# GNN and FFN kernel: the tail's residual arithmetic moved from GpSimd to VectorE, LayerNorm 4 put into the tile loop

## The chip, the core and the metric

The kernel runs on one core of one Trainium2 chip. The core has a TensorE (matrix products, called PE in the profile), a VectorE (DVE), a ScalarE (ACT), a GpSimd (POOL) and a SyncE that issues transfers (SP). The metric is the device time of one execution in microseconds (us). The engines run their own instruction streams in order and meet only at semaphores, so an engine that waits also holds up everything that stands behind the wait in its own stream.

## What is computed

6250 nodes of 256 features pass four steps, each with a residual: a weighted sum over 106250 edges, a mixture of experts, a two-layer graph convolution and a feed-forward network on the best-scored half of the nodes. The change lies in the second convolution's product, its LayerNorm (called LN5 here), and what the last step needs ahead of its network:

```
h = _gcn_conv(x, src, dst, W1, b1); h = relu(h)
h = _gcn_conv(h, src, dst, W2, b2)      # (segment sum) @ W2, * deg_in**-0.5, + b2
h = _layer_norm(h, gamma, beta)         # LN5
x = x + h                               # residual
n = _layernorm(x)                       # LN4
weights = n @ wr + br                   # router score of each node
idx = top_k(weights, k)                 # half of the nodes
x = x + (n, plus y * score for the chosen rows, y = ffn(n))
```

The reference reads "x = x + L1_ffn(n)" with "processed + n" inside, so the output of a node that is not chosen is x + n.

## The kernel before

The nodes lie as 49 tiles (T) of 128 rows in seven chunks (NCH) of seven tiles (CH). X is the residual stream, 128 x 49 x 256 in SBUF (in reg_a). ACC (in reg_b) is 128 x 49 x 257: 256 features and one column that counts edges.

**The convolutions** (tags p1 and p2) work block by block: GpSimd gathers the rows of 128 edges with an indirect DMA (`gathers`, L629, 831 of them for each convolution, into a ring of 24 slots), SyncE relays the arrivals, ScalarE makes one-hot matrices (L787, L797), TensorE multiplies (L1780) into eight PSUM banks in turn, and VectorE adds the result to its tile of ACC (L1324 in `item_sums`, 880 items).

**The tile loops** (tags c1 and c2) follow each convolution: for each tile TensorE transposes ACC (L1690), ScalarE copies the transposed tile out of PSUM (`evacuate`, L755), TensorE multiplies with the weights (L1700), and VectorE scales by the degree and adds the bias (`product`, L1448). In c1 ScalarE applies relu (L809) and SyncE writes the rows to HBM, from where p2 gathers them. GpSimd may start p2's gathers only when all of these rows are written. Ahead of c1 VectorE takes the edge counts (L1441) and inverts their square root.

**The tail** is everything from c2 to the router scores WV. LN5 is spread over VectorE (`ln_stats` L843 and L846, `ln_scale` L851 to L870) and ScalarE (`ln_std` L684, `ln_apply` L693) chunk by chunk within the c2 loop. GpSimd then multiplies the chunk by gamma (L664) and adds it to X (L666); it had added beta to the whole of X between the gathers of p1 and p2 (L655). After the loop LN4 runs in the same way over X, GpSimd adds the normalized chunk to X for the output (L670), and VectorE takes the 49 score products with the router's weights (L1482), plus the bias (L1484). A search for the threshold, the inversion of the selection, and the network follow (L1498 onwards).

The order on every engine is the order of the code. What sets it around the change are the positions `t % CH` in the loops at which the pieces of a LayerNorm are issued.

Of the kernel before, what the change touches and what calls it, by code (L numbers as in the profile page):

```python
# [14 lines left out]
P = 128  # L15
ALU = mybir.AluOpType
# [37 lines left out]
def gnn_program(nc, x, src, dst, edge_weight, Wr, br, ln_g, ln_b, W1, b1, W2, b2,  # L54
# [6 lines left out]
    KC = D // P  # L61
# [39 lines left out]
    with ExitStack() as ctx:  # L101
# [145 lines left out]
        gws = tb[:, 0:2 * KC * D].rearrange("p (l c d) -> p l c d", l=2, c=KC)  # L247
        GB1B, GB2B, GAMB, BETB, FB2B, FWRB = (tb[:, 2 * KC * D + k * D:2 * KC * D + (k + 1) * D] for k in range(6))
# [35 lines left out]
        CNTS = sm(7)  # L284
        EDGE = sm(3).bitcast(I32)
# [117 lines left out]
        def _(sp):  # L403
# [88 lines left out]
            for l, a in enumerate((gW1, gW2)):  # L492
                sp.dma_start(gws[:, l, :, :], a.rearrange("(c p) d -> p c d", p=P)).then_inc(z("tail_in"), 16)
            for to, a in ((GB1B, gb1), (GB2B, gb2), (GAMB, gamma), (BETB, beta), (FB2B, fb2)):
                sp.dma_start(to, row1(a, D)).then_inc(z("tail_in"), 16)
# [44 lines left out]
        def _(pool):  # L540
# [92 lines left out]
            def chunk(c):  # L633
                w_ = slice(c * CH, (c + 1) * CH)
                return X[:, w_, :], ACC[:, w_, 0:D]


# [15 lines left out]
            pool.wait_ge(z("tail_in"), 8 * 16)  # L653
            pool.wait_ge(*norms("ln3", "norm", NCH))
            g.tensor_tensor(X, X, per_column(BETB, T), ALU.add).then_inc(z("beta_in"), 1)  # L655
# [3 lines left out]

            pool.wait_ge(z("beta_in"), 1)  # L660
            for c in range(NCH):
                x_, h = chunk(c)
                pool.wait_ge(*norms("ln5", "norm", c + 1))
                g.tensor_tensor(h, h, per_column(GAMB, CH), ALU.mult).then_inc(z("scaled"), 1)  # L664
                pool.wait_ge(z("scaled"), c + 1)
                g.tensor_tensor(x_, x_, h, ALU.add).then_inc(z("x3_set"), 1)  # L666
            for c in range(NCH):
                x_, h = chunk(c)
                pool.wait_ge(*norms("ln4", "norm", c + 1))
                g.tensor_tensor(x_, x_, h, ALU.add).then_inc(z("sum_set"), 1)  # L670
# [7 lines left out]
        def _(act):  # L678
# [135 lines left out]
            for t in range(T):  # L814
                if t + 1 < T:
                    evacuate("c2", t + 1)
                c = t // CH - 1
                if c >= 0 and t % CH == 2:
                    ln_std("ln5", c)
                if c >= 0 and t % CH == 5:  # L820
                    ln_apply("ln5", c, *[lambda i: ACC[:, c * CH + i, 0:D]] * 2)
# [1037 lines left out]
```

## Time and profile before

| what | us |
|---|---|
| runs | 5300.11, 5294.97, 5300.14 (median 5300.11) |
| profiled execution | 5287.03 |
| its span, first to last instruction | 5285.4 |
| busy: PE, DVE, ACT, POOL | 3767.5, 2195.0, 1831.9, 2937.5 |

Around the span lie 1.6 us of the profiled execution. The profiled execution is 13.1 us (0.25%) under the median of the three runs. The page gives busy time by engine, the costliest groups of instructions (line, engine, operation, names and shapes, then busy time, mean ns of one, and idle time just before), and the chain that ended last. The places of this change were read from the timeline (start, duration, engine, line, with the idle time before in brackets and what ended it) and from the table of stretches.

### The profile page before, as it was taken

To read this page: it belongs to the slowest core of one execution; us is meant where nothing else is said; L and a number is where in the kernel's file an instruction comes from. 1 tells how busy PE (TensorE), PEld (TensorE's weight loads), DVE (VectorE), ACT (ScalarE), POOL (GpSimd) and SP (SyncE) were. 2 spreads that over 40 slices of the span, in tenths; PEclk is the share of its full clock that TensorE was granted. 3 is DMA by queue.
4 is the path that set the end of the run, shared out by engine and by line. 5 is a ranking of instruction groups with operands and counts; after the bars stand their busy time and mean duration, and the time that the engine had idled before them with its cause. 6 is when DMAs were issued, how large, how long until landed. Compare 5 with 4: busy or idle time off the path is not lost.

```text
span 5285.4 us, 63030 instructions
## 1 busy us (share of the span) xinstructions
PE 3767.5 (71%) x14313; PEld 2762.7 (52%) x14313; DVE 2195.0 (42%) x6079; ACT 1831.9 (35%) x4499; POOL 2937.5 (56%) x2860
## 2 busy tenths in 40 slices
PE   1666668986886999999566666666666666666178
PEld 0444447765666688888433443333433433345167
DVE  8543336665775411111333333334433333334831
ACT  5333333332003522222344444443444444443331
POOL 0677777776000133333277777777377777775413
PEclk9888889998996999999767777777877778778579
DMA  2334347776886244444533333333233333332212
GB/s 80 117 123 124 122 137 244 243 244 200 251 249 217 65 109 111 116 108 109 143 108 106 105 106 106 105 106 96 88 106 106 106 105 106 105 105 68 97 22 31
DMA packets 322627, 660.22 MB, mean 125 GB/s; under 512 B 60683, under 2 KB 142923, under 8 KB 322150
## 3 DMA queue, kind: packets, MB, share of 16 engines
q0 software_dynamic: 148960, 365.25, 23.9%
q1 hardware_dynamic: 173318, 290.95, 18.5%
q8 instruction: 142, 2.33, 0.2%
q14 instruction: 207, 1.70, 0.1%
HBM read 488.94 MB, written 174.87 MB: 126 GB/s over the span
## 4 chain that ended last, share of the span: by engine, by line
POOL 30%; issue 10%; PE 6%; DVE 3%; DMA 1%; ACT 1%; SPq 0%; POOLq 0%; DVEq 0%; ACTq 0%
POOL work L629 30%; PE bank L1728 2%; PE bank L1700 2%; PE bank L1739 2%; DVE small L843 0%; DMA conv_rows<-work 0%; DVE work L1482 0%; PE bank L1761 0%; DVE small L1441 0%; PE bank L1690 0%; DVE work L1516 0%; ACT reg_b L693 0%; SPq L491 0%; DMA out_dram<-work,slot_t 0%; ACT work L693 0%
## 5 line engine op out<-in xcount | busy, mean ns | idle before, releaser
L1780 PE MATMUL bank<-work,reg_a 128*128 x3520 | 1349.7, 528 | 808.5 <-DVE reg_b L1324 359.4
L629 POOL DMA_INDIRECT work<-conv_rows,tables x1662 | 1571.6, 946 | 618.1 <-issue 505.7
L1780 PEld LDWEIGHTS bank<-work,reg_a 128*128 128x128 f32 x3520 | 820.1, 254 | 1338.1 <-issue 1220.7
L1324 DVE TENSOR_TENSOR reg_b<-reg_b,bank 128x257 f32 x1760 | 744.2, 423 | 1336.1 <-PE bank L1780 1232.8
L590 POOL DMA_INDIRECT messages<-work,small x880 | 883.0, 1003 | 292.7 <-issue 184.5
L797 ACT ACTIVATE reg_a<-reg_a,ones 128x512 f32<-128x512 f32 x440 | 317.7, 722 | 1155.5 <-PE bank L1780 1155.1
L1639 PE MATMUL bank<-reg_b,reg_a 128*128 x1760 | 539.4, 449 | 242.1 <-ACT work L720 216.8
L720 ACT ACTIVATE work<-bank,tables 128x256 f32<-128x256 f32 x880 | 387.2, 473 | 784.7 <-PE bank L1639 387.4
L787 ACT ACTIVATE reg_a<-iota,tables 128x128 f32<-128x128 f32 x1760 | 562.5, 391 | 31.3 <-DVEq L1457 12.8
L1639 PEld LDWEIGHTS bank<-reg_b,reg_a 128*128 128x128 f32 x1760 | 352.3, 218 | 376.2 <-issue 334.6
L611 POOL DMA_INDIRECT residual_rows<-work,slot_t x112 | 177.8, 1588 | 478.8 <-DVE work L1303 306.6
L601 POOL DMA_INDIRECT work<-expert_in_rows,slot_t x112 | 111.8, 998 | 526.1 <-DVEq L1265 473.4
L1728 PE MATMUL bank<-work,reg_a 128*128 128x256 f32 x1792 | 397.8, 381 | 2.5 <-DVE work L1285 2.5
L1652 PE MATMUL bank<-reg_b,reg_a 128*128 128x257 f32 x1544 | 369.7, 387 | 27.8 <-DVE reg_a L1185 27.7
L1728 PEld LDWEIGHTS bank<-work,reg_a 128*128 128x128 f32 x1792 | 342.1, 191 | 49.3 <-DVE work L1285 3.1
L1652 PEld LDWEIGHTS bank<-reg_b,reg_a 128*128 128x128 f32 x1544 | 291.4, 192 | 90.0 <-DVE reg_a L1185 49.6
L747 ACT ACTIVATE work<-bank,param_t 128x256 f32<-128x256 f32 x280 | 117.3, 470 | 362.7 <-PE bank L1728 362.6
L747 ACT ACTIVATE tables<-bank,param_t 128x256 f32<-128x256 f32 x272 | 114.0, 470 | 359.6 <-PE bank L1728 359.6
L1195 DVE TENSOR_TENSOR reg_a<-reg_a,bank 128x257 f32 x514 | 215.6, 419 | 47.1 <-PE bank L1652 29.0
L1185 DVE TENSOR_TENSOR reg_a<-iota,tables 128x512 f32<-128x512 f32 x257 | 177.8, 692 | 102.2 <-PE bank L1652 76.7
L1285 DVE TENSOR_SCALAR work<-bank,param_t 128x256 f32<-128x256 f32 x112 | 55.8, 539 | 345.5 <-PE bank L1715 345.4
L1739 PE MATMUL bank<-reg_b,tables 128*128 x896 | 198.0, 379 | 0.0
(341 smaller groups left out, 3745.0 us busy)
## 6 DMA issues: line engine op xcount, KB each, us to landing
reg_b<-messages SPq DMA_DIRECT2D x386, 258.0 KB, 3.5
reg_a<-in_L_ffn_W_dram SPq DMA_DIRECT2D x56, 1024.0 KB, 5.3
b_rows<-messages SPq DMA_DIRECT2D x128, 258.0 KB
reg_a<-item_rows SPq DMA_DIRECT2D x110, 256.0 KB, 3.8
work<-conv_rows,tables POOLq DMA_INDIRECT x1662, 2.7
messages<-work,small POOLq DMA_INDIRECT x880
conv_rows<-work SPq DMA_DIRECT2D x14, 896.0 KB, 4.0
reg_b<-in_L_ffn_W_dram SPq DMA_DIRECT2D x8, 1024.0 KB, 11.8
```

Source lines behind the costliest of these rows:

```text
L590: g.indirect_dma_start(msgs, bass.IndirectOffsetOnAxis(ap=PIDX[:, i % 32:i % 32 + 1], axis=0), G[:, u, :], None, bounds_check=BASE2 + E2 - ...
L629: g.indirect_dma_start(GC[:, u, 0:D], None, table, bass.IndirectOffsetOnAxis(ap=BSRC[:, b_:b_ + 1], axis=0)).then_inc(z(f"conv_in{u // 4}" ...
L720: a.activation(G[:, u, 0:D], ps[i % 3][:, 0:D], ACT.Copy, scale=WT[:, i:i + 1]).then_inc(z("m_row"), 1)
L747: a.activation(HT[j % 2][:, k, :], ps[1 + k // 2][:, k % 2 * PP:(k % 2 + 1) * PP], gelu, bias=PT[:, bass.ds(col, 1)]).then_inc(z("net_gelu ...
L787: ins = a.activation(DIST[:, k % 8, :], IOTA[:], ACT.Abs, bias=DREL[:, k:k + 1], scale=-1.0)
L797: a.activation(OHP[:, i % OHR:i % OHR + 4, :], DIST[:, i % 8:i % 8 + 4, :], ACT.Relu, scale=-1.0, bias=ONES[:, 0:1]).then_inc(z("conv_oh"), 4)
L1324: v.tensor_tensor(acc, acc, ps[i % 8][:, 0:D + 1], ALU.add).then_inc(z("conv_add"), 1)
L1639: pe.matmul(ps[i % 3][:, 0:D], OHT[:, i % 8, :], XNf[:, bass.ds(offs[k], D)], start=True, stop=True).then_inc(z("m_mm"), 1)
L1652: pe.matmul(ps[sum_bank(pr)][:, 0:D + 1], SOH[:, q % 2 * 4 + b_, :], QG[q % 4][:, b_, 0:D + 1], start=(k == 0), stop=(k == 1)).then_inc(z( ...
L1728: ins = pe.matmul(ps[1 + k // 2][:, k % 2 * PP:(k % 2 + 1) * PP], w_, XE[:, c, :], start=(c == 0), stop=(c == KC - 1))
L1739: ins = pe.matmul(ps[5 + j % 2][:, h * D:(h + 1) * D], HT[j % 2][:, k, h * P:(h + 1) * P], w_, start=(k == 0), stop=(k == HC - 1))
L1780: pe.matmul(ps[i % 8][:, 0:D + 1], OHP[:, i % OHR, :], GCf[:, bass.ds(offs[i % 4], D + 1)], start=True, stop=True).then_inc(z(f"{tag}_mm"), 1)
```

## The change

Beta is now added by VectorE, one tile at a time, inside the c1 loop. Gamma and the residual add are now done by VectorE, one chunk at a time, inside the c2 loop. LN4 runs two chunks behind the products in that same loop, which has two more rounds of seven steps. x + n, which is x (1 + r) - mean r, is one ScalarE activation per tile (`sums`) in place of GpSimd's add. The scores are no longer taken from the normalized rows. They are assembled from parts: an extra 257th weight column (W2 times gamma times wr, summed) gives the score part of h out of the c2 product, and X times wr is summed per tile. The 55 VectorE steps that make these parts (`score_parts`) are placed in `item_sums` of p2, one after every eighth item.

```
-            g.tensor_tensor(X, X, per_column(BETB, T), ALU.add).then_inc(z("beta_in"), 1)
...
-                g.tensor_tensor(h, h, per_column(GAMB, CH), ALU.mult).then_inc(z("scaled"), 1)
-                g.tensor_tensor(x_, x_, h, ALU.add).then_inc(z("x3_set"), 1)
...
-                g.tensor_tensor(x_, x_, h, ALU.add).then_inc(z("sum_set"), 1)
```

ScalarE:

```
+            def sums(c):
+                for t in range(c * CH, (c + 1) * CH):
+                    ins = a.activation(X[:, t, :], X[:, t, :], ACT.Identity, bias=NB[:, 1, t:t + 1], scale=RS1[:, t:t + 1])
+                ins.then_inc(z("sum_set"), 1)
+            for t in range((NCH + 2) * CH):
                 if t + 1 < T:
                     evacuate("c2", t + 1)
+                c5, c4, at = t // CH - 1, t // CH - 2, t % CH
+                if 0 <= c5 < NCH and at == 0:
+                    ln_std("ln5", c5)
+                if 0 <= c5 < NCH and at == 1:
+                    ln_apply("ln5", c5, *[lambda i: ACC[:, c5 * CH + i, 0:D]] * 2)
+                if c4 >= 1 and at == 3:
+                    sums(c4 - 1)
+                if c4 >= 0 and at == 4:
+                    ln_std("ln4", c4, 1)
+                if c4 >= 0 and at == 6:
+                    ln_apply("ln4", c4, ...)
```

VectorE:

```
+            def score_parts():
+                step(v.tensor_tensor(GFB, GAMB, FWRB, ALU.mult))
+                for c in range(KC):
+                    step(v.scalar_tensor_tensor(DUMP, GW2X[:, c, 0:D], 1.0, GFB, ALU.mult, ALU.mult,
+                                                accum_out=GW2X[:, c, D:D + 1]))
...
+                for t in range(T):
+                    step(v.scalar_tensor_tensor(DUMP, X[:, t, :], 1.0, FWRB, ALU.mult, ALU.mult, accum_out=WV[:, t:t + 1]))
+                    yield
...
+                    if side is not None and i % 8 == 6:
+                        next(side, None)
...
+                v.tensor_tensor(X[:, t, :], X[:, t, :], BETB, ALU.add).then_inc(z("beta_in"), 1)
...
+            for t in range((NCH + 2) * CH):
+                if t < T:
+                    product("c2", D + 1, t, ACC[:, t, :], GB2X).then_inc(z("lin2"), 1)
+                c5, c4, at = t // CH - 1, t // CH - 2, t % CH
+                if 0 <= c5 < NCH:
+                    if at == 0:
+                        ln_stats("ln5", c5, lambda i: ACC[:, c5 * CH + i, 0:D])
+                    if at == 1:
+                        ln_scale("ln5", c5)
+                if c4 >= 0:
+                    if at == 0:
+                        residual(c4)
+                    if at == 2:
+                        step(v.tensor_tensor(X[:, w_, :], X[:, w_, :], ACC[:, w_, 0:D], ALU.add))
+                    if at == 3:
+                        ln_stats("ln4", c4, lambda i: X[:, c4 * CH + i, :], 1)
+                    if at == 5:
+                        ln_scale("ln4", c4, 1, plus_one=RS1)
```

`residual(c)` waits for LN5's applied chunk c and multiplies it by gamma. The order on GpSimd between the gathers, before (L655 is the beta add, L664 and L666 the first of gamma and residual):

```order
L629 DMA work<-conv1_rows,tables 128x256 x831
L655 TENSOR_TENSOR reg_a<-reg_a,reg_b 128x49x256
L629 DMA work<-conv2_rows,tables 128x256 x831
L664 TENSOR_TENSOR reg_b<-reg_b 128x7x256
L666 TENSOR_TENSOR reg_a<-reg_a,reg_b 128x7x256
```

and now:

```order
L633 DMA work<-conv1_rows,tables 128x256 x831
L633 DMA work<-conv2_rows,tables 128x256 x831
L605 DMA work<-ffn_in_rows,slot_t 128x256 x8
```

GpSimd computes nothing any more between the first gather of p1 and the network. On VectorE, the step from one chunk to the next in the c2 loop before (L1448 is the product, L843 and L846 LN5's statistics, L862 to L870 its scale):

```order
L1448 SCALAR_TENSOR_TENSOR reg_b<-bank5,small,reg_b 128x256
L843 BN_STATS small<-reg_b 128x6 x7
L846 BN_AGGR small<-small 128x2 x7
L1448 SCALAR_TENSOR_TENSOR reg_b<-bank2,small,reg_b 128x256
```

and one whole chunk of the c2 loop now (L1463 is the product, L1481 gamma, L1498 the residual add, L860 one plus the scale; L832 with reg_b is LN5's statistics, with reg_a LN4's):

```order
L1463 SCALAR_TENSOR_TENSOR reg_b<-bank3,small,reg_b 128x257
L832 BN_STATS small<-reg_b 128x6 x7
L835 BN_AGGR small<-small 128x2 x7
L1481 TENSOR_TENSOR reg_b<-reg_b 128x7x256
L1463 SCALAR_TENSOR_TENSOR reg_b<-bank4,small,reg_b 128x257
...
L1463 SCALAR_TENSOR_TENSOR reg_b<-bank5,small,reg_b 128x257
L1498 TENSOR_TENSOR reg_a<-reg_a,reg_b 128x7x256
L1463 SCALAR_TENSOR_TENSOR reg_b<-bank2,small,reg_b 128x257
L832 BN_STATS small<-reg_a 128x6 x7
L835 BN_AGGR small<-small 128x2 x7
```

Gamma, the residual add and LN4 have moved between the products, and the product of a tile waits its turn behind them. In p2 a side step (L1312) now stands between two of VectorE's item adds (L1336):

```order
L1336 TENSOR_TENSOR reg_b<-reg_b,bank6 128x257
L1312 SCALAR_TENSOR_TENSOR reg_b<-reg_b 128x256
L1336 ISA
L1336 TENSOR_TENSOR reg_b<-reg_b,bank7 128x257
```

One such step follows every eighth add, 55 in all, so they end at item 440 of 880.

## Rows read from the trace of the kernel before

**Rows 1.** The page's costliest groups: GpSimd's gathers of both convolutions

```profile
L629 POOL DMA_INDIRECT work<-conv_rows,tables x1662 | 1571.6, 946 | 618.1 <-issue 505.7
```

**Rows 2.** Table of stretches: us, busy (x) of PE, PEld, DVE, ACT, POOL, granted clock, DMA

```profile
3716.00:3777.00 61.00, 58.75 (x277) 43.82 (x275) 22.72 (x47) 36.21 (x94) 0.00 (x0) 1.00 0.27 91
4700.00:4825.00 125.00, 79.94 (x222) 50.63 (x222) 46.52 (x110) 43.45 (x108) 90.76 (x96) 0.80 0.36 103
...
4845.00:4852.00 7.00, 5.97 (x16) 4.74 (x17) 3.73 (x16) 2.29 (x7) 6.05 (x2) 0.51 0.00 0
4852.00:4910.00 58.00, 39.71 (x191) 31.91 (x189) 34.34 (x133) 29.31 (x71) 32.76 (x10) 0.94 0.00 1
4910.00:4999.00 89.00, 0.00 (x0) 0.00 (x0) 85.53 (x245) 29.76 (x64) 42.63 (x11) 0.50 0.42 144
```

**Rows 3.** Timeline (start, us, engine, line) where p1 ends and c1 begins

```profile
3685.94 24.51 POOL L655 TENSOR_TENSOR reg_a<-reg_a,reg_b 128x12544 f32<-128x12544 f32 x1
...
3691.76 18.76 DVE L1441 TENSOR_SCALAR small<-reg_b 128x49 f32<-128x49 f32 x1
```

**Rows 4.** Timeline of the c1 loop: two products, and p2's first gather

```profile
3719.17 0.48 DVE L1448 SCALAR_TENSOR_TENSOR work<-bank,small,reg_b 128x256 f32<-128x256 f32 x1 [0.70 <-PE bank L1700]
...
3720.57 0.48 DVE L1448 SCALAR_TENSOR_TENSOR work<-bank,small,reg_b 128x256 f32<-128x256 f32 x1 [0.91 <-PE bank L1700]
...
3781.30 0.97 POOL L629 DMA_INDIRECT work<-conv_rows,tables  x1 [70.85 <-DMA conv_rows<-work]
```

**Rows 5.** Timeline of the message stage: GpSimd's DMA issues beside VectorE's operations

```profile
903.00 0.56 DVE L1108 TENSOR_TENSOR reg_a<-reg_a,work 128x392 f32<-128x392 f32 x1
...
910.31 0.41 DVE L1195 TENSOR_TENSOR reg_a<-reg_a,bank 128x257 f32 x1
910.36 0.97 POOL L590 DMA_INDIRECT messages<-work,small  x1 [0.30 <-issue]
...
911.26 0.69 DVE L1185 TENSOR_TENSOR reg_a<-iota,tables 128x512 f32<-128x512 f32 x1
911.63 1.17 POOL L590 DMA_INDIRECT messages<-work,small  x1 [0.30 <-issue]
```

**Rows 6.** Timeline of the c2 loop, around the first two LN5 chunks

```profile
4825.18 0.42 DVE L1324 TENSOR_TENSOR reg_b<-reg_b,bank 128x257 f32 x1 [0.20 <-DVE reg_b L1324]
...
4835.74 2.37 DVE L843 BATCH_NORM_STATS2 small<-reg_b 128x6 f32<-128x256 f32 x7
...
4838.64 1.23 DVE L1448 SCALAR_TENSOR_TENSOR reg_b<-bank,small,reg_b 128x256 f32<-128x256 f32 x3
...
4840.94 0.19 DVE L862 RECIPROCAL small<-small 128x7 f32<-128x7 f32 x1
...
4842.18 3.55 ACT L693 ACTIVATE reg_b<-reg_b,small 128x256 f32<-128x256 f32 x7 [1.04 <-DVE small L870]
...
4846.03 2.08 PE L1700 MATMUL bank<-reg_b,work 128*128 128x256 f32 x4 [3.13 <-ACT work L755]
...
4859.93 1.13 PE L1700 MATMUL bank<-reg_b,work 128*128 128x256 f32 x4 [3.14 <-ACT work L755]
```

**Rows 7.** VectorE's groups from 4825.6 to 4999: busy us, mean ns

```profile
L1482 DVE SCALAR_TENSOR_TENSOR work<-reg_b 128x256 f32<-128x256 f32 x49 | 28.1, 573 | 1.7
...
L870 DVE SCALAR_TENSOR_TENSOR small<-small 128x7 f32<-128x7 f32 x14 | 20.6, 1470 | 0.5
...
L853 DVE TENSOR_SCALAR small<-small 128x7 f32<-128x7 f32 x14 | 9.7, 692 | 0.5
```

**Rows 8.** Timeline of GpSimd and of VectorE in LN4: one add beside one scale

```profile
4933.05 3.97 POOL L670 TENSOR_TENSOR reg_a<-reg_a,reg_b 128x1792 f32<-128x1792 f32 x1 [4.09 <-ACT reg_b L693]
```

```profile
4933.23 3.81 DVE L870 SCALAR_TENSOR_TENSOR small<-small 128x7 f32<-128x7 f32 x1
```

**Rows 9.** Timeline of VectorE at the end of the tail

```profile
4968.68 0.42 DVE L1482 SCALAR_TENSOR_TENSOR work<-reg_b 128x256 f32<-128x256 f32 x1
...
4998.84 0.25 DVE L1484 TENSOR_SCALAR small<-small,brb 128x49 f32<-128x49 f32 x1
```

More of the change, by code:

```diff
@@ L813, in _ @@
             evacuate("c2", 0)
[L814 removed]
+            def sums(c):
[3 more added lines that the diff above has]
+            for t in range((NCH + 2) * CH):
                 if t + 1 < T:
                     evacuate("c2", t + 1)
[L817 to L821, printed above, removed]
[L822 to L829 removed]
+                c5, c4, at = t // CH - 1, t // CH - 2, t % CH
[8 more added lines that the diff above has]
+                if c4 >= 0 and at == 6:
+                    ln_apply("ln4", c4, lambda i: X[:, c4 * CH + i, :], lambda i: ACC[:, c4 * CH + i, 0:D], 1)
+            sums(NCH - 1)
             scale_onehots("ffn", NFT, T, lambda s, t: WV[:, t:t + 1])
@@ L869, in ln_scale @@
                     step(v.tensor_tensor(r, r, extra[:, w_], ALU.mult))
+                if plus_one is not None:
+                    v.tensor_scalar(plus_one[:, w_], r, 1.0, None, ALU.add)
                 v.scalar_tensor_tensor(n, MV[:, s, w_, 0], -1.0, r, ALU.mult, ALU.mult).then_inc(norms(tag, "scale")[0], 1)
@@ L1444, in _, with product @@
             v.wait_ge(z("tail_in"), 8 * 16)
-            def product(tag, l, t, to, bias):
+            v.wait_ge(*norms("ln3", "norm", NCH))
+            def product(tag, width, t, to, bias):
                 v.wait_ge(z("tile_mm"), t + 1 + TILES_BEFORE[tag])
-                return v.scalar_tensor_tensor(to, ps[2 + t % 4][:, 0:D], DI[:, t:t + 1], bias, ALU.mult, ALU.add)
+                return v.scalar_tensor_tensor(to, ps[2 + t % 4][:, 0:width], DI[:, t:t + 1], bias, ALU.mult, ALU.add)
             for t in range(T):
@@ L1457, in _ @@
             v.engine_nop().then_inc(z("conv_ready"), 1)
-            item_sums("p2")
+            item_sums("p2", score_parts())
             v.wait_ge(z("conv_add"), 2 * NI)
-            for t in range(T):
-                product("c2", 1, t, ACC[:, t, 0:D], GB2B).then_inc(z("lin2"), 1)
-                c = t // CH - 1
-                if c >= 0 and t % CH == 0:
-                    v.wait_ge(z("lin2"), (c + 1) * CH)
-                    ln_stats("ln5", c, lambda i: ACC[:, c * CH + i, 0:D])
-                if c >= 0 and t % CH == 4:
-                    ln_scale("ln5", c)
@@ L1487, in _ @@
+            step(v.scalar_tensor_tensor(T1, MV[:, 1, :, 0], MINUS_F, WV, ALU.mult, ALU.add))
+            step(v.tensor_tensor(T1, T1, RS[:, 1, :], ALU.mult))
+            step(v.tensor_scalar(WV, T1, FBR, None, ALU.add))
             ROUND = [0]
```

83 lines of the change are left out of this document (36 added, 47 removed).

## Prediction

> **What bounds the kernel now.** I read the costliest groups first, then the table of stretches, then the timeline at the three places that the change touches. The convolutions are bound by GpSimd: a gather is busy 946 ns and 505.7 us of issue gaps are spread over 1662 of them, so (1571.6 + 505.7) / 1662 = 1.25 us each, without a wait on anything else [rows 1]. VectorE has room there: 46.5 us busy in 125 [rows 2].
>
> At the end of p1 the reader should see a 49-column operation of VectorE, L1441, that takes 18.76 us, while GpSimd's addition of beta runs from 3685.94 for 24.51 us. Both end at 3710.5 [rows 3]. An operation of this width takes 0.25 us elsewhere (L1484) [rows 9]. It stands ahead of c1, whose rows p2's gathers wait for (70.85 us idle) [rows 4], so its length is on the path.
>
> The tail runs from the last item add, which ends at 4825.60 [rows 6], to the score bias at 4998.84 [rows 9]: 173.2 us. The same collision is in it. An LN4 scale started at 4933.23, 0.18 us behind GpSimd's add, and ended with it [rows 8]. A seven-column operation needs under 0.2 us (L862: 0.19) [rows 6] and a score product 0.42 [rows 9]. With 0.17 for the first kind the stall is L870 20.6 - 2.4 = 18.2, L853 9.7 - 2.4 = 7.3, L1482 28.1 - 20.6 = 7.5, together 33 us [rows 7].
>
> **The change part by part.**
>
> *Beta leaves GpSimd.* L1441 falls from 18.76 to about 0.25 us: **-18.5 us**, and all of c1 and p2 moves up by it. What is late next is the reciprocal chain and the first copy, which came right behind L1441 anyway. GpSimd's own gathers do not wait less, since c1's rows release them.
>
> *Beta on VectorE, 49 adds of 128x256 in c1.* From 0.56 us for 392 columns and 0.69 for 512, both with two SBUF inputs [rows 5], one column costs 1.1 ns and 256 columns cost 0.41 us. c1's products start 1.40 and 1.18 us apart and take 0.48 [rows 4], and the cycle is product, relu, copy, TensorE. 0.48 + 0.41 = 0.89 us fits into the shorter step, so this costs **0**; VectorE ends c1 0.4 us later, but p2's first gather needs the written rows only. Uncovered it would be 20 us.
>
> *The 55 side steps in p2.* VectorE has the time. The danger is GpSimd. An issue that began at 911.63, inside an operation of VectorE with two SBUF inputs (911.26 to 911.95), took 1.17 us in place of 0.97; one that began at 910.36 inside an operation with one input in PSUM took 0.97 [rows 5]. p2's own adds are of the second kind, 53 of the side steps of the first. A gather starts inside a 0.42 us step one time in three (0.42 / 1.25), and then loses half of it less 0.1, so 53 x 0.05 = **+3 us**. The low bound is 0, where no start falls inside; the high one is 53 x 0.42 = 22, where each does.
>
> The Trainium skill, "SBUF — State Buffer", "Who interferes with whom", says that a two-input `tensor_tensor` takes only the read interface of the shared ports, that descriptor generation needs the write interface, and so (inferred, it says) that DMA issue is not stalled. By that rule this term would be 0; the stretched issue speaks against it.
>
> *The tail.* No arithmetic of GpSimd is left beside VectorE, so the 33 us of stalls go, and so do the 49 score products (4968.68 to 4998.84, 30 us, of which 7.5 are stall [rows 7, 9]). In exchange VectorE gets 14 operations of 128x1792. At 0.56 + 1400 x 1.1 ns that is 2.05 us each (GpSimd took about 4 [rows 8]); an upper end is 2.4, if all of the 512-column row's 0.69 us scaled with the width, and a lower one 1.8, if a tenth of the slope is lost to overlap. The walk below moves by +3 and -2 us between them, since the residual add stands beside a wait.
>
> I walked through one full chunk of the new order, with 0.4 us for a product (three take 1.23), 2.9 for statistics (2.37 plus the seven small ones), 1.1 for a scale (4840.94 until ScalarE starts at 4842.18, less 0.1), 3.55 for seven applied tiles, and 1.13 + 0.4 us for TensorE and the copy [rows 6]:
> - product 0.4, LN5 statistics 2.9, gamma 2.05, product 0.4, LN5 scale 1.1: 6.9 us
> - ScalarE has meanwhile stopped at `ln_apply`, and the copies of the coming tiles stand behind it. Two products were ready and the residual add (2.05) runs beside it; then VectorE waits: apply 3.55, copy and TensorE 1.5, about 5.1 us from the scale to the next product
> - product 0.4, LN4 statistics 2.9, product 0.4, wait 0.4, product 0.4, LN4 scale 1.2, product 0.4, wait 0.3: 6.4 us
>
> That is 18.4 us a chunk, of which VectorE waits 3.7 or so; before, the products behind two applies in turn were 13.9 us apart (4846.03 to 4859.93). The loop has 10.1 us for chunk 0 as before (4825.60 to 4835.74), 14.5 for chunk 1 (LN5 only, its scale now holds the copies early), 4 x 18.4 + 17.5 for the next five, 14.7 for round 7 (no products: statistics twice 2.9, gamma and add 4.1, scales 2.3, 2.5 of waiting for ScalarE's `apply` and `sums`), 9.5 for round 8, and 0.8 for the last three small operations: **141 us** with TensorE at the full clock. The same walk of the old order, with GpSimd's operations holding VectorE, gives 172.6 against the 173.2 seen, so I trust it to a few us.
>
> *TensorE's clock.* The tile products took 1.13 us at 4859.93 and 2.08 at 4846.03 [rows 6], the latter in a stretch at 0.51, behind a wait of 3.13 us. From 4852 to 4910 the granted clock was 0.94 with TensorE busy 68%, in the convolution 0.80 at 64% [rows 2]. In the new loop TensorE has 7 x 1.13 = 7.9 us of work in 18.4, or 43%. At the half level throughout the walk gives 168 us, since each of a chunk's three waits for a tile grows by about 1 us and chunk 0 by 8. I take a mixture, full in the first chunk and half in about half of the others: **148 us, so -25**.
>
> Sum: -18.5 + 0 + 3 - 25 = -40.5, so 5287.0 - 40.5 = 5246.5 for an execution like the profiled one. The median of the runs is 13.1 us above it, so 5300.1 - 40.5 = **5259.6, say 5259**.
>
> **The rivals.**
> - *Full clock in the tile loop*: 141 us, gain 18.5 + 32 - 3, time 5252, down to 5243 if the big operations are at their low end. For it: 1.00 in c1 at dense work [rows 2]. Against it: TensorE's idle stretches of 3 to 6 us in each chunk.
> - *Half clock in the tile loop*: 168 us, gain 18.5 + 5 - 3, time 5280. For it: the stretch at 0.51; against it: the next wait of 3.14 us was followed by a product at 1.13.
> - *The side steps hold up GpSimd for whole issues*: the end on the other side. If VectorE's two-input step and a gather take turns so that each step costs GpSimd one gather of 1.25 us, the 53 cost 66 us, and the time is 5300.1 - 43.5 + 66 = 5323. It decides from 43.5 / 53 = 0.82 us a step. Against it: the stretched issue lost 0.20 us, and VectorE's operation in progress there had its usual 0.69 [rows 5]. A milder form, 0.3 us for each, gives 5273.
> - *The new loop eats the gain*: if GpSimd's share only moves to VectorE at GpSimd's price (4 us for each of the 14), the chunk grows by 4 us, the tail is 168 to 176, and the time 5282 to 5290. Against it: the 1.1 ns a column.
>
> **How the numbers follow.** The mixed clock (5253 to 5270) 0.5; full clock or better (5240 to 5253) 0.2; half clock or a mild side cost (5270 to 5287) 0.2; GpSimd's price 0.04; whole issues lost 0.04; the rest 0.02. The range takes the first three but their outer ends: 5241 to 5283. About 0.2% (10.6 us) can be told from no change; the L1441 stall alone is worth more. Faster 0.91, same 0.05, slower 0.04.
>
> **What would show it.** L1441's successor at 0.25 us, c1 starting within 1 us of the last item add, and c1's products still 2.58 us apart by twos. GpSimd's gathers in the first half of p2 at 1.25 us with some at 1.1 to 1.4; p2 from first gather to last item add 3 us longer than 4825.6 - 3781.3 = 1044.3. Rounds of 18 to 20 us in the c2 loop, with VectorE's longest wait for TensorE behind each LN5 apply; no VectorE operation of seven columns over 0.2 us; last item add to score bias 141 to 155 us; everything behind as before. I am wrong if c1 shows products further apart, if 128x1792 takes over 2.4 us, or if the granted clock in the loop is 0.5.

## The result, and the profile after

The changed kernel took 5253.43 us (median of 4, 5242.20 to 5255.98) and the kernel before, run beside it, 5298.39 (5294.97 to 5300.14). The ratio is 0.9913 with a 95% interval of 0.9899 to 0.9928: 45.0 us less, where 40.5 were predicted; the time itself was put at 5259 us, in a range of 5241 to 5283. The profiled execution has a span of 5240.6 us against 5285.4, 44.8 less. The two traces divide it like this (each stretch by its first and last rows):

| stretch | before | after | difference | predicted |
|---|---|---|---|---|
| start to the end of p1's last item add | 3691.72 | 3691.11 | -0.6 | 0 |
| from there to c1's first product | 21.67 | 2.30 | -19.4 | -18.5 |
| c1, first product to last | 62.55 | 61.93 | -0.6 | 0 |
| to p2's first gather | 5.36 | 5.35 | 0 | 0 |
| p2, first gather to last item add | 1044.30 | 1046.97 | +2.7 | +3 |
| last item add to the start of the score bias | 173.24 | 147.19 | -26.1 | -25 |
| the rest | 286.5 | 285.8 | -0.8 | 0 |

The first and the last row, which the change doesn't touch, show that two executions differ by some 0.8 us in such a stretch anyway. GpSimd is less busy and TensorE, VectorE and ScalarE about as much as before. The gathers still bound the convolutions, at the same cost of issue. First the page of the kernel after, busy time by engine (us) and the group of the gathers, which answers to [rows 1]:

```profile
PE 3780.5 (72%) x14313; PEld 2766.9 (53%) x14313; DVE 2181.9 (42%) x6165; ACT 1853.8 (35%) x4548; POOL 2837.6 (54%) x2838
...
L633 POOL DMA_INDIRECT work<-conv_rows,tables x1662 | 1574.0, 947 | 622.3 <-issue 505.7
```

**The end of p1.** The timeline after (start, us, engine, line) answers to [rows 3] and [rows 4]; L1455 is the operation that was L1441, L1463 the product and L1468 the beta add:

```profile
3691.15 0.20 DVE L1455 TENSOR_SCALAR small<-reg_b 128x49 f32<-128x49 f32 x1
...
3692.13 1.13 PE L1726 MATMUL bank<-reg_b,work 128*128 128x256 f32 x4 [0.24 <-ACT work L739]
...
3693.41 0.48 DVE L1463 SCALAR_TENSOR_TENSOR work<-bank,small,reg_b 128x256 f32<-128x256 f32 x1 [0.27 <-PE bank L1726]
3693.81 0.41 DVE L1468 TENSOR_TENSOR reg_a<-reg_a,reg_b 128x256 f32<-128x256 f32 x1
```

```profile
3760.69 0.94 POOL L633 DMA_INDIRECT work<-conv_rows,tables  x1 [75.41 <-DMA conv_rows<-work]
```

The 49-column operation takes 0.20 us where it took 18.76, and c1 starts at once. The beta add takes the 0.41 us that was worked out from [rows 5], and the products of c1 are still 2.58 us apart by twos (3716.61, 3719.19, 3721.77). GpSimd's idle time before p2 is longer than in [rows 4] (75.41 against 70.85) because it now has nothing to compute there.

**The side steps in p2.** In the timeline after, three of GpSimd's gathers and one side step (L1312) that the middle one started inside:

```profile
3796.00 0.95 POOL L633 DMA_INDIRECT work<-conv_rows,tables  x1 [0.30 <-issue]
...
3797.18 0.42 DVE L1312 SCALAR_TENSOR_TENSOR reg_b<-reg_b 128x256 f32<-128x256 f32 x1
3797.25 1.17 POOL L633 DMA_INDIRECT work<-conv_rows,tables  x1 [0.30 <-issue]
...
3798.72 0.95 POOL L633 DMA_INDIRECT work<-conv_rows,tables  x1 [0.30 <-issue]
```

From 3760 to 4310, the half with side steps, 16 of 438 gathers took 1.01 to 1.17 us, and each of these started inside a side step with two SBUF inputs; in the same half of the kernel before the longest gather took 0.97. Together the 16 are 2.4 us over 0.947 each. How long each took follows from where in the step of 0.42 us it started: 0.07 us in it took 1.17 us, 0.14 in 1.09 to 1.10, 0.23 in 1.01, and the five that started 0.28 us in or later took 0.94 to 0.95. That is what a gather looks like that is held until about 0.3 us after the start of the step, 0.1 before its end, as the prediction assumed. The 16 include the one `tensor_tensor` among the side steps (L1309): a gather that started 0.11 us into it took 1.13.

**The c2 loop.** One round of seven steps runs from one gamma multiplication (L1481) to the next. The timeline after, with one LN5 apply (L677), answers to [rows 6]:

```profile
4837.37 2.00 DVE L1481 TENSOR_TENSOR reg_b<-reg_b 128x1792 f32<-128x1792 f32 x1
...
4856.70 1.99 DVE L1481 TENSOR_TENSOR reg_b<-reg_b 128x1792 f32<-128x1792 f32 x1
...
4860.36 3.55 ACT L677 ACTIVATE reg_b<-reg_b,small 128x256 f32<-128x256 f32 x7 [2.98 <-DVE small L861]
4860.64 2.02 DVE L1498 TENSOR_TENSOR reg_a<-reg_a,reg_b 128x1792 f32<-128x1792 f32 x1
4863.81 0.62 ACT L739 COPY work<-bank 128x256 f32<-128x256 f32 x2
...
4864.21 2.08 PE L1726 MATMUL bank<-reg_b,work 128*128 128x257 f32 x4 [5.43 <-ACT work L739]
...
4866.41 0.49 DVE L1463 SCALAR_TENSOR_TENSOR reg_b<-bank,small,reg_b 128x257 f32<-128x257 f32 x1 [3.76 <-PE bank L1726]
```

ScalarE applies LN5 to seven tiles, the copy of the next tile stands behind it, TensorE has been idle for 5.43 us and runs that tile at 2.08 us in place of 1.13, and VectorE waits 3.76 us for it. VectorE's groups from 4838 to 4986 (busy us, mean ns) answer to [rows 7]:

```profile
L1498 DVE TENSOR_TENSOR reg_a<-reg_a,reg_b 128x1792 f32<-128x1792 f32 x7 | 14.1, 2018 | 0.0
L1481 DVE TENSOR_TENSOR reg_b<-reg_b 128x1792 f32<-128x1792 f32 x7 | 14.0, 1996 | 0.0
...
L842 DVE TENSOR_SCALAR small<-small 128x7 f32<-128x7 f32 x13 | 2.2, 170 | 0.4
```

The wide operations take 2.00 and 2.02 us, half of what one took on GpSimd [rows 8]. L842, which was L853 with a mean of 692 ns, takes 170: no seven-column operation is held up any more. Table of stretches after (us, busy (x) of PE, PEld, DVE, ACT, POOL, granted clock), which answers to [rows 2]:

```profile
3693.40:3755.40 62.00, 58.33 (x285) 44.74 (x284) 39.27 (x97) 36.54 (x95) 0.00 (x0) 1.00 0.27 90
...
4833.00:4851.00 18.00, 9.87 (x38) 7.30 (x36) 13.36 (x43) 5.85 (x16) 0.00 (x0) 0.72 0.01 1
4851.00:4870.00 19.00, 10.50 (x42) 8.05 (x42) 14.23 (x50) 12.65 (x30) 0.00 (x0) 0.82 0.20 69
4870.00:4889.00 19.00, 11.83 (x39) 9.18 (x40) 14.23 (x50) 12.80 (x30) 0.00 (x0) 0.73 0.27 92
```

c1 ran at full clock, the c2 loop at 0.72 to 0.82 in these stretches. The tail ends with the score bias, which answers to the last line of [rows 9]:

```profile
4954.85 0.25 DVE L1510 TENSOR_SCALAR small<-small,brb 128x49 f32<-128x49 f32 x1
```

### The profile page after: what moved, and what is told of

The parts are those of the page before. It is cut to its first block and busy times, and to the rows that moved or that the text cites. A ratio compares the mean times of both kernels' runs of the same rounds, so it can differ in the third digit from the quotient of the medians.

```text
span 5240.6 us, 63145 instructions
## 1 busy us (share of the span) xinstructions
PE 3780.5 (72%) x14313; PEld 2766.9 (53%) x14313; DVE 2181.9 (42%) x6165; ACT 1853.8 (35%) x4548; POOL 2837.6 (54%) x2838
## 5 line engine op out<-in xcount | busy, mean ns | idle before, releaser
L1336 DVE TENSOR_TENSOR reg_b<-reg_b,bank 128x257 f32 x1760 | 744.1, 423 | 1319.2 <-PE bank L1806 1212.0
L1678 PE MATMUL bank<-reg_b,reg_a 128*128 128x257 f32 x1544 | 371.6, 388 | 26.1 <-DVE reg_a L1176 26.0
## 6 DMA issues: line engine op xcount, KB each, us to landing
reg_b<-in_L_ffn_W_dram SPq DMA_DIRECT2D x8, 1024.0 KB, 11.8
```

The lines of the kernel that those rows point to most:

```text
L1336: v.tensor_tensor(acc, acc, ps[i % 8][:, 0:D + 1], ALU.add).then_inc(z("conv_add"), 1)
L1678: pe.matmul(ps[sum_bank(pr)][:, 0:D + 1], SOH[:, q % 2 * 4 + b_, :], QG[q % 4][:, b_, 0:D + 1], start=(k == 0), stop=(k == 1)).then_inc(z( ...
```

## The experiments

The kernels ran in three groups, each with the kernel before beside it: 5291.7 us in the first, 5901.28 in the second, 5859.33 in the third. In the last two the convolutions were slower (GpSimd also waited for free ring slots), so times are compared within a group only. The result above is a measurement apart. "Tail" below is the time from the last item add to the end of the score bias: 173.5 us before, 147.4 after. It contains no gathers and differs less between the groups: of the kernels with the order of the changed one, e3, e4 and e10 of the last two groups have 148.7 to 149.6.

### Beta: who holds up whom

**e1_beta_only** (first group) is the kernel before with nothing changed but beta:

```
-            g.tensor_tensor(X, X, per_column(BETB, T), ALU.add).then_inc(z("beta_in"), 1)
...
                 product("c1", 0, t, ZB[:, t % 2, :], GB1B).then_inc(z("lin1"), 1)
+                v.tensor_tensor(X[:, t, :], X[:, t, :], BETB, ALU.add).then_inc(z("beta_in"), 1)
```

> The kernel before with one part of the change alone: beta is added by VectorE in c1, tile by tile, and GpSimd keeps gamma, residual and the last add. Theory (the 18.76 us of L1441 were GpSimd's one long addition): the edge-count operation takes 0.2 us, c1 starts right behind the last item add, the time falls by 18 to 20 us, ratio to before 0.9964. The tail stays at 173 us. Rival (the gain at this place in the changed kernel came from less work elsewhere): under 5 us.

Measured: 5272.41 us, 0.9962 [0.9948, 0.9975], 19.3 us less. The 49-column operation took 0.20 us, the tail 172.7. Beta alone is worth what the first term of the sum said.

**e2_beta_pieces** (first group) leaves beta on GpSimd, in 49 pieces:

```
-            g.tensor_tensor(X, X, per_column(BETB, T), ALU.add).then_inc(z("beta_in"), 1)
+            for t in range(T):
+                g.tensor_tensor(X[:, t, :], X[:, t, :], BETB, ALU.add).then_inc(z("beta_in"), 1)
```

> The kernel before with GpSimd's addition of beta cut into 49 additions of 128x256. The work stays on GpSimd and still overlaps VectorE; only the length of one instruction changes. Theory (GpSimd holds the port for one instruction at a time, and VectorE gets in between): the edge-count operation waits at most one piece, 0.6 us, and the time falls by 15 to 20 us, ratio about 0.9966, although GpSimd needs longer for the whole, some 30 us. Rival (VectorE is slow or starved as long as GpSimd computes at all): it still takes over 10 us, and the gain is under 8 us.

Measured: 5298.19 us, 1.0011 [1.0002, 1.0020], 6.5 us more than before, about as much as the pieces take longer together than one addition (31.26 against 24.51). It was to wait for one piece and waited for all. The timeline of GpSimd and of VectorE in this kernel:

```profile
3690.66 31.26 POOL L656 TENSOR_TENSOR reg_a<-reg_a,reg_b 128x256 f32<-128x256 f32 x49
```

```profile
3696.59 25.39 DVE L1442 TENSOR_SCALAR small<-reg_b 128x49 f32<-128x49 f32 x1
```

The pieces take 31.26 us and VectorE's operation, begun 5.9 us in, ends with the last of them. The Trainium skill, "SBUF — State Buffer", "SBUF: two separate sides", has it that the one of the two that starts first keeps the shared ports for the whole instruction. Read as one instruction at a time, that would have let VectorE in after one piece, 0.64 us (31.26 / 49); in this trace the end of an instruction is not enough when the next one is ready.

**e9_beta_waits** (third group) is e2 with a wait between the pieces:

```
                 g.tensor_tensor(X[:, t, :], X[:, t, :], BETB, ALU.add).then_inc(z("beta_in"), 1)
+                pool.wait_ge(z("beta_in"), t + 1)
```

> The kernel before with GpSimd's beta in 49 additions, and GpSimd waiting on a semaphore for each before it issues the next. In the version without these waits VectorE's edge-count operation was held for 25.39 us, until the last of the 49. Theory (VectorE gets the port only where GpSimd has nothing issued, which a wait gives): the edge-count operation takes under 1.2 us, c1 starts 1 to 2 us behind the last item add, the time falls by 15 to 19 us, ratio 0.9968. Rival (VectorE's operation is served last whatever GpSimd's queue looks like): again over 20 us, ratio 1.000 or more.

Measured: 5855.81 us, 0.9995 [0.9986, 1.0004]. The mechanism came out, the time did not: the interval is from 8 us faster to 2 us slower. GpSimd and VectorE in its timeline:

```profile
4090.87 0.95 POOL L629 DMA_INDIRECT work<-conv_rows,tables  x1 [0.30 <-issue]
4091.83 37.33 POOL L656 TENSOR_TENSOR reg_a<-reg_a,reg_b 128x256 f32<-128x256 f32 x49
```

```profile
4109.77 0.34 DVE L1443 TENSOR_SCALAR small<-reg_b 128x49 f32<-128x49 f32 x1
```

In the midst of the pieces VectorE's operation takes 0.34 us. Three small operations behind it still took 0.66 to 0.77 us in place of 0.21, about a piece each, but c1's first product came 3.69 us after the last item add, as in e10 and e12 (3.49), which have no beta on GpSimd. The stall is gone. But look at when GpSimd was done with its gathers: here its last one was issued at 4090.87, 18.9 us ahead of the end of the last item add (4109.74). In the first trace before, beta began at 3685.94 and the last add ended at 3691.72, 5.8 us later [rows 3]. An undivided beta add of 24.5 us would have ended at 4116.3 here and held VectorE for 6.6 us, not 18.8. By the same sum e10, e11 and e12 of this group, whose last item add ended 15.5 to 17.9 us after the last gather of p1 had, would have stalled for 6.6 to 9 us. So some 6 to 9 us were to be had and not 15 to 19, and the measured time is compatible with that, as it is with no gain at all. That the kernel before stalls for so long under these conditions is worked out, not seen: its trace was not taken there. The whole times can't decide it either. With 6.4 us of stall saved and the shortening of the tail from 174.0 us in e9, e10, e11 and e12 would gain 31, 41 and 49 us on the kernel before; they gained 28.8, 38.4 and 55.3.

### The side steps in p2

**e3_no_sums** (second group) is the kernel after without the 49 sums of X times the router weights; that part is left out of the scores.

```
-                for t in range(T):
-                    step(v.scalar_tensor_tensor(DUMP, X[:, t, :], 1.0, FWRB, ..., accum_out=WV[:, t:t + 1]))
-                    yield
+                v.memset(WV, 0.0)
+                yield
```

> The changed kernel without the 49 sums of x times the router's weights in p2; the scores therefore lack that part. Theory (a gather whose issue starts inside such a step loses some 0.15 us): p2 from first gather to last item add falls from 1047.0 to 1044.5 us, no gather in its first half over 1.0 us, the time falls by 2 to 3 us. Rival (the steps cost nothing on the path): 1047.0 stays.

**e4_sums_x4** (second group) and **e10_sums_x4** (third, the same kernel again) issue each of them four times:

```
                 for t in range(T):
+                    for _ in range(4):
                         step(v.scalar_tensor_tensor(DUMP, X[:, t, :], 1.0, FWRB, ..., accum_out=WV[:, t:t + 1]))
```

> The changed kernel with each of the 49 sums done four times in its place, 196 operations. Theory (a start inside an operation with two SBUF inputs is held until its end, less 0.1 us): one gather start in three falls into each, p2 grows by 147 x 0.05 = 7 to 8 us, to 1054 to 1055. First rival (two-input operations do not hold up DMA issue): p2 stays at 1047. Second rival (VectorE and GpSimd take turns, a whole issue is lost per operation): 1047 + 147 x 1.25 = over 1200.

> Again the changed kernel with each of the 49 sums of p2 done four times, to see it where gathers come every 1.25 us without waiting for ring slots. In the changed kernel 16 of 438 gathers in this half took 1.01 to 1.17 us and the 438 together 2.8 us more than at 0.947. Theory (a start in three falls inside a step): 55 to 70 of them stretched, the 440 gathers together 8 to 10 us more than at 0.947, p2 1052 to 1055 us against 1047.0. Rival (back to back the four are one block that a gather start meets once): about 4 us more, p2 1048 to 1049.

GpSimd's gathers in the first half of p2 in e3, e4 and e10 (busy us, mean ns, idle before and why):

```profile
L633 POOL DMA_INDIRECT work<-conv_rows,tables x454 | 429.2, 945 | 316.5 <-issue 134.1 <-SPq L516 91.7 <-DMA conv_rows<-work 90.7
```

```profile
L633 POOL DMA_INDIRECT work<-conv_rows,tables x444 | 423.6, 954 | 307.6 <-issue 125.1 <-SPq L516 93.6 <-DMA conv_rows<-work 88.9
```

```profile
L633 POOL DMA_INDIRECT work<-conv_rows,tables x471 | 452.0, 960 | 311.9 <-issue 135.4 <-SPq L516 88.7 <-DMA conv_rows<-work 87.7
```

Without sums the mean is 945 ns and none is above 0.97 us. With four times as many, it is 954 and 960: 27 and 34 gathers took 0.98 to 1.19 us, together 3.7 and 5.4 us over 0.947 each. The whole excess in e10, 440 gathers at 0.960 in place of 0.947, is 5.9 us, where 8 to 10 were expected (the rival had 4). So the steps do stretch gathers, and a side step never costs a whole issue. How much four times the steps cost can't be compared with the 16 gathers of the kernel after, which ran under other conditions. In the groups of e4 and e10 the kernels with single sums had 1 (e6), 4 (e8), 2 (e11) and 6 (e12) gathers over 0.975 us, and only 5 to 11 that started inside a step, where e4 and e10 had 62 and 59. There the cost grew more than fourfold. Not all of those 62 and 59 were stretched: many started 0.28 us or more into a step, as the five above, and some in its first 0.04 us.

Medians and lengths say less: 5863.54 us (0.9943 [0.9928, 0.9959]) for e3, 5874.85 (0.9952 [0.9937, 0.9967]) for e4, with p2 1216.7 and 1221.3 us long. But e6 below, with the single sums, has 1221.7 in the same group and e8 1217.2, so 4 us there are scatter. In the third group e10 (5830.56 us, 0.9951 [0.9936, 0.9967]) has 1210.1, as have e12 with single sums (1210.2) and e9 with none (1210.0), where 1052 to 1055 were expected for conditions without that wait: where GpSimd waits for ring slots anyway (SPq L516, some 90 us here), stretched issues vanish in the wait. In the first conditions it has no such wait, and p2 is 1044.3, 1045.6 and 1045.4 us without side steps (before, e1, e2) and 1047.0, 1046.9 and 1047.9 with them (after, e5, e7): 2.2 us between the means. In e5 18 gathers of 20 that started inside a step were stretched, in e7 25 of 30, by the same 1.24 us less the distance from the start of the step. The one of these that started early in a step and was not stretched (0.15 us in, e7) had met a `tensor_reduce`, which has one SBUF input.

### The place of LayerNorm 4

**e7_ln4_behind** (first group) is the kernel after with LN4 taken out of the c2 loop and put behind it, chunk by chunk, with the sums x + n:

```
                 if 0 <= c5 < NCH and at == 1:
                     ln_apply("ln5", c5, ...)
-                if c4 >= 1 and at == 3:
-                    sums(c4 - 1)
-                if c4 >= 0 and at == 4:
-                    ln_std("ln4", c4, 1)
-                if c4 >= 0 and at == 6:
-                    ln_apply("ln4", c4, ...)
+            for c in range(NCH + 1):
+                if c < NCH:
+                    ln_std("ln4", c, 1)
+                if c >= 1:
+                    ln_apply("ln4", c - 1, ...)
+                    sums(c - 1)
```

> The changed kernel with LN4 and the last add behind the c2 loop instead of in it (everything still without GpSimd). Theory (taking GpSimd out and putting LN4 into the loop each earn a share, since LN4's small steps and its waits for ScalarE only hide beside products): tail from last item add to score bias 164 us at TensorE's full clock in the loop, 172 with the mixture seen, against 147.4 in the changed kernel and 173.5 before, so 15 to 27 us slower than the changed kernel, ratio to before about 0.996. Rival (all of the tail's gain is the end of the stalls and of the score products; the place of LN4 is worth nothing): ratio 0.9913 as the changed kernel, tail 145 to 150.

Measured: 5280.18 us, 0.9976 [0.9967, 0.9985]; the tail is 177.7, more than the 172 expected and 4.2 more than before. The stretch behind its loop (columns as above):

```profile
4951.00:4995.00 44.00, 0.00 (x0) 0.00 (x0) 27.80 (x148) 37.80 (x81) 0.00 (x0) 0.50 0.56 196
```

Alone, LN4 is bound by ScalarE: two applications of 3.55 us for each chunk, 37.8 us busy in 44. And the loop hardly gets shorter for its absence: from the first gamma operation at 4847.28 to the sixth at 4938.71 are 18.3 us a round, against 19.1 with LN4 in it (at a granted clock of 0.72 there and 0.79 here), and VectorE is idle for 37.0 of these 91.4 us, against 23.2 of 95.7. Up to the seventh gamma operation 9.1 us are saved, behind it 39.3 are added (49.6 in place of 10.3). So LN4 is nearly free inside the loop, where the engines wait for each other, and its place is worth 30 us of the tail. The whole gain of the tail hangs on it: with the arithmetic moved to VectorE but LN4 behind, nothing is gained in the tail on the kernel before, and the 11.5 us that the kernel is faster are beta's 19 less this and the side steps, to about 1 us.

### What bounds a round

**e8_filler** (second group) gives TensorE eight unread products in the gap that the LN5 apply leaves, and nothing else:

```
                 tile_products("c2", t, D + 1, lambda c: GW2X[:, c, :], 2 + t % 4, 0)
+                if t >= CH and t % CH == 2:
+                    for _ in range(8):
+                        pe.matmul(ps[7][:, 0:D], IDENT[:], FILL, start=True, stop=True)
```

> The changed kernel with eight products of 128x256 into an unused PSUM bank behind the third tile of each chunk, where TensorE waits 5.4 us for the copies that stand behind LN5's apply. They are extra work of 3.5 us at the full clock, with no one waiting for them. Theory (TensorE runs the two tile products behind this gap at the lower clock because it has idled): the product behind the apply takes 1.13 in place of 2.08 us, a round 18.4 in place of 19.3, the tail 141 to 144 us in place of 147.4. Rival (the lower clock comes from the sparse work of the whole stage, not from this gap): the fillers run at the lower clock too, take 7 us and delay the next tile, tail 150 to 158.

Measured: 5860.77 us, 0.9945 [0.9928, 0.9963]; the tail is 142.4, against 148.7 and 149.6 in e3 and e4 of the same group. TensorE in its timeline, where the product of [5.43 <-ACT work L739] stood at 2.08 us (L1851 is the filler, L1727 the tile product):

```profile
5455.47 3.62 PE L1851 MATMUL bank<-b_rows,ident 128*128 128x256 f32 x16
...
5461.28 1.14 PE L1727 MATMUL bank<-reg_b,work 128*128 128x257 f32 x4 [1.98 <-ACT work L740]
```

And the loop's stretch in e8, then in e3:

```profile
5450.00:5557.00 107.00, 64.35 (x284) 50.58 (x283) 85.37 (x294) 68.90 (x158) 0.00 (x0) 0.90 0.23 80
```

```profile
5450.00:5557.00 107.00, 53.87 (x198) 40.14 (x195) 82.81 (x284) 66.78 (x154) 0.00 (x0) 0.77 0.23 78
```

Idle for 1.98 us in place of 5.43, TensorE runs the awaited tile at full clock, and the granted clock of the loop is 0.90 in place of 0.77. Not every tile is at full clock: at 5490.37 one still took 2.08 us. The gamma operations start at 5453.76, 5472.14, 5490.52: 18.38 us a round. That is the prediction's walk at full clock (18.4).

**e5_apply_late** (first group) moves ScalarE's LN5 apply from step 1 of a round to step 4, so that the copies of three more tiles go ahead of it:

```
-                if 0 <= c5 < NCH and at == 1:
-                    ln_apply("ln5", c5, ...)
                 if c4 >= 1 and at == 3:
                     sums(c4 - 1)
+                if 0 <= c5 < NCH and at == 4:
+                    ln_apply("ln5", c5, ...)
```

> The changed kernel with ScalarE's LN5 apply issued at position 4 of a chunk's seven, behind four copies, instead of at position 1. Nothing else moves. Theory (VectorE's longest wait, 3.8 us a round, is for tiles whose copies stand behind the apply on ScalarE): the wait goes, a round takes 15.5 to 17 us in place of 19.3, the tail 124 to 135 us in place of 147.4, ratio to before 0.988. Rival (the apply's result becomes late for gamma, or LN4's apply and the sums take its place as the blocker): tail 143 or more, ratio 0.991.

Measured: 5233.06 us, 0.9886 [0.9871, 0.9901], 58.6 us less than before; the tail is 134.6, at the upper end of what was expected, and a round takes 17.3 us, a little more. Between the first and the sixth gamma operation VectorE waits for tile products for 9.1 us, where it waited 21.0 in the kernel after.

**e6_order** (second group) and **e12_order** (third, the same kernel again) order the round once more:

```
 ScalarE
-  step 1: ln_apply("ln5", c5)   step 3: sums(c4 - 1)           step 4: ln_std("ln4", c4, 1)
+  step 2: sums(c4 - 1)          step 3: ln_apply("ln5", c5)    step 5: ln_std("ln4", c4, 1)
 VectorE
-  step 2: X += h                step 5: ln_scale("ln4", c4, 1, plus_one=RS1)
+  step 1: X += h                step 4: ln_scale("ln4", c4, 1, plus_one=RS1)
```

> The changed kernel with a new order: on ScalarE the sums at position 2, LN5's apply at 3, LN4's root at 5; on VectorE the residual add at 1, right behind LN5's scale, and LN4's scale at 4. Theory (with the copies ahead of the applies VectorE's own work, some 15.5 us a round, is the bound): tail 122 to 134 us, 0 to 3 us under the kernel with the late apply alone, ratio to before 0.9875. Rival: as slow as the changed kernel, since each order only moves the wait to another apply.

> The new order of the loop alone, again, on the same chip as the version with fillers: tail 131 us (131.2 was seen), 16 us under the changed kernel, ratio to before 0.9880. If the late apply alone (tail 134.6, ratio 0.9886) is all that counts, the two cannot be told apart by their times.

Measured: e6 5852.76 us, 0.9913 [0.9899, 0.9928], tail 131.2; e12 5804.08 us, 0.9904 [0.9888, 0.9920], tail 131.2. The tail came out; the ratios are behind the 0.9875 and 0.9880 expected, which go by e5's 0.9886 in the first group; by the sum under e9, beta's part is smaller here. The timeline of e12 at an LN5 apply:

```profile
5419.44 3.55 ACT L677 ACTIVATE reg_b<-reg_b,small 128x256 f32<-128x256 f32 x7
...
5421.38 0.88 DVE L1463 SCALAR_TENSOR_TENSOR reg_b<-bank,small,reg_b 128x257 f32<-128x257 f32 x2
5422.90 0.61 ACT L739 COPY work<-bank 128x256 f32<-128x256 f32 x2
...
5423.30 1.14 PE L1726 MATMUL bank<-reg_b,work 128*128 128x257 f32 x4 [1.89 <-ACT work L739]
```

VectorE has two products to work on while ScalarE applies, TensorE idles 1.89 us in place of 5.43 and runs that tile at full clock; others in this loop still took 2.08 us. From the first gamma operation to the sixth, five rounds take 81.5 us (5415.78 to 5497.23), 16.3 each, against 19.1 after, 17.3 in e5 and 18.3 in e8, and VectorE's wait for tile products in them is 4.6 us, against 21.0, 9.1 and 15.7. So most of what LN5's apply costs is the order in which ScalarE finds its work, and less of it is the clock. What e12 gains on e5 is not split up: three pieces of ScalarE's work and two of VectorE's lie elsewhere.

**e11_order_filler** (third group) puts the two together: e6 with three filler products behind the tile products of steps 0 and 6.

```
+                if t >= CH and t % CH in (0, 6):
+                    for _ in range(3):
+                        pe.matmul(ps[7][:, 0:D], IDENT[:], FILL, start=True, stop=True)
```

> The new order of the loop (sums at 2, LN5 applied at 3, residual add at 1, LN4's scale at 4) with three unread products of 128x256 on TensorE behind the first and the last tile of each chunk. Theory (here VectorE's own 15.5 us of work a round is the bound and the lower clock costs it 1 to 1.5 us a round): round 15.5 to 16.2 in place of 16.9 us, tail 124 to 129 us against 131.2 without, ratio to before 0.9865. Rival (the fillers stand ahead of tiles that are waited for): tail 131 or more, ratio as the order alone.

Measured: 5820.90 us, 0.9930 [0.9916, 0.9943]; the tail is 139.8, 8.6 us longer than e12's. TensorE and VectorE in its timeline (L1464 is the product on VectorE):

```profile
5440.79 1.46 PE L1851 MATMUL bank<-b_rows,ident 128*128 128x256 f32 x6
5442.08 0.38 PE L1717 MATMUL bank<-ident,reg_b 128*128 128x128 f32 x2
5442.30 1.03 PE L1727 MATMUL bank<-reg_b,work 128*128 128x257 f32 x4
```

```profile
5443.37 0.48 DVE L1464 SCALAR_TENSOR_TENSOR reg_b<-bank,small,reg_b 128x257 f32<-128x257 f32 x1 [1.90 <-PE bank L1727]
```

The fillers stand ahead of a tile that VectorE is waiting for. The granted clock of the loop is 0.83 with them (5420 to 5530) and was 0.82 without (5410 to 5510): they bought next to no clock, and a round takes 17.8 us in place of 16.3, as the rival of that expectation had it.

## Why the prediction was right

**Beta (-18.5, measured -19.4).** The operation fell to 0.20 us as predicted, and e1 shows it alone. The 0.8 us that were missed are TensorE's. In the timeline before, its first tile product of c1 stood behind the stall:

```profile
3711.17 2.07 PE L1700 MATMUL bank<-reg_b,work 128*128 128x256 f32 x4 [18.66 <-ACT work L755]
```

Now it comes after 0.24 us and takes 1.13. The granted clock was 0.56 from 3710 to 3716 before, and is 1.00 from 3691 to 3700 after. That the clock comes back with the end of the stall was not in the sum.

**Beta in c1 (0, measured 0).** The products stay 2.58 us apart by twos, and each add of 0.41 us lies in VectorE's wait. c1 is 0.6 us shorter, for the same reason as above.

**Side steps (+3, measured +2.7).** The rule was right, the figure worked out from it was not. One start in three, each losing half of 0.42 us less 0.1, is 0.11 / 3 = 0.04 us a step and 2.0 us for 53, not 0.05 and 3. Measured were 21 starts inside a step where 18 were expected, which lost 0.12 us each, 2.4 together. So the slip and the chance of three more starts brought +3 near to the 2.7 seen; over the six traces of the first conditions the difference is 2.2. The rule of the Trainium skill that stood beside this term in the prediction ("SBUF — State Buffer", "Who interferes with whom"; a two-input `tensor_tensor` doesn't stall DMA issue) would have made it 0. The gather of 1.13 us that started inside the one `tensor_tensor` step, and the 15 beside `scalar_tensor_tensor` steps, decide against it here.

**The tail (-25, measured -26.1).** The walk, by its parts, with the number in e8, where TensorE mostly keeps its clock:

| stretch (from the last item add, by gamma operations) | walk, full clock | after | e8 |
|---|---|---|---|
| to the first gamma | 27.9 | 29.7 | 29.1 |
| first to sixth | 90.7 | 95.7 | 91.3 |
| sixth to seventh | 11.8 | 11.7 | 11.7 |
| seventh to the end of the score bias | 10.3 | 10.3 | 10.3 |
| sum | 140.7 | 147.4 | 142.4 |

The walk missed the loop at (nearly) full clock by 1.7 us in 141. Of the 7 us allowed for the clock, 5.0 are the difference of the two columns, 6.3 to 7.2 the difference of e8 to e3 and e4 beside it. Where they arise is not quite what was assumed. The mixture was full clock in the first chunk and half in about half of the others; the granted clock was 0.88 from 4808 to 4837, and 1.8 us were lost up to the first gamma operation. By the prediction's own figures (8 of the 27 us between full and half clock lie in chunk 0) that mixture comes to 141 + 19 / 2 = 150.5 us, and not to the 148 that were written and met by 147.4. The 7 us were an estimate that came out, not a sum. The wide operations at 2.00 and 2.02 us (2.05 assumed) settle the rival in which they keep GpSimd's price. The wait of 3.76 us behind an LN5 apply is about what the walk had for a whole round (3.7); in the trace VectorE is idle for 4.6 us a round, 4.2 of them for tile products.

**What it did not see.** Beside the sum, it took the order of the round as given. e5, e6 and e12 show that the wait that it named as VectorE's longest was avoidable, and worth 12.8 us of the tail in e5 (147.4 to 134.6) and 17.5 in e6 (against e3's 148.7). And its first term holds only for the conditions of its own trace: by e9's rows the stall would be 6.6 in place of 18.8 us where GpSimd has finished its gathers earlier.

**The rivals.** Whole issues lost to side steps: not seen, not even with four times the steps. Full clock throughout: not seen; nearest to it is e8, 0.90 with TensorE's gap filled. Half clock throughout: not seen; 0.72 to 0.82. GpSimd's price for the wide operations: not seen; its time, 5282 to 5290 for a tail of 168 to 176, was 3 us high by the terms of the prediction's own sum (5300.1 - 18.5 + 3 - 5.2 = 5279 for 168).

The best orders tried are those of e5 and of e12. e12's tail is 18 us shorter than that of e10 in the same group, which has the order of the kernel after (131.2 against 149.2), and its runs (5798 to 5809 us) lie below all of e10's (5829 to 5833) and e11's (5809 to 5827). Against the kernel before, e5 took 0.9886 where after took 0.9913, with intervals that just touch (up to 0.9901, from 0.9899). Which of the two is the better was not run side by side; by tails it is e12 (131.2 against 134.6).

## What to carry to other kernels

Where two engines collide on a short operation, price the stall by how long the other one still works when the short one starts, in the trace of the conditions that count; it is not a property of either operation. When work goes into a loop in which engines already wait for each other, walk one round through all engines: it can be nearly free there (30 us here), and the walk also names the operation that holds everybody else's next piece, which is then the next thing to move. A filler for the clock paid in a gap that is there anyway (6.8 us of tail in e8) and cost 8.6 us ahead of tiles that are awaited (e11).

## What the hardware showed beyond that

- 49 operations of GpSimd back to back held VectorE's 49-column operation to the end of the last one (25.39 us), as one undivided operation did (18.76). With a semaphore wait behind each piece VectorE was through in 0.34 us.
- A gather that starts inside an operation of VectorE with two SBUF inputs is stretched, from 0.947 us to up to 1.19. If it starts 0.06 to 0.24 us into a step of 0.42 us it takes about 1.24 us less that distance; from 0.28 us in, it is not stretched (5 of 21 in the kernel after).
- A 128x1792 operation of float32 in SBUF takes 2.00 us (multiplication) and 2.02 (addition) on VectorE. On GpSimd, in the kernel before, the multiplication took 3.62 to 3.73 us and the addition 3.97 to 3.99.
- The idle time just before a tile product doesn't settle its clock. Behind 5.43 us it took 2.08 us and behind 1.98 and 1.89 it took 1.14, but behind 2.77 us, in the kernel after, one took 2.08 (4838.10) and one 1.14 (4821.46), and in the kernel before one took 2.08 behind 3.13 and one 1.13 behind 3.14 [rows 6]. What decides was not tried apart.
